# Eight stages of a graph and expert network on one core: beginnings of the stages rearranged

## The reference

```
x = x + gnn0(layernorm(x));  x = x + ffn0(layernorm(x))     # graph convolution; 8 experts, top 2, capacity 187
x = x + gnn1(layernorm(x));  x = x + ffn1(layernorm(x))     # graph attention, batch norm; 8 experts, top 1
x = x + gnn2(layernorm(x));  x = x + ffn2(layernorm(x))     # two attention layers; one expert merged from 8
x = x + gnn3(layernorm(x));  x = x + ffn3(layernorm(x))     # mean of neighbours; 32 experts, each takes its 39 best rows
```

## Time and profile before

| | us |
|---|---|
| median of 3 runs (3417.18 to 3420.14) | 3418.47 |
| the profiled execution | 3384.64 |
| its span, first to last instruction | 3382.9 |
| PE busy | 2479.7 (73%) |
| DVE busy | 1791.0 (53%) |
| ACT busy | 774.3 (23%) |
| POOL busy | 615.5 (18%) |

### The profile page before, as it was taken

How to read it: one execution, slowest core, us unless ns; L and a number is a source line. 1 busy time by engine, 2 the same in 40 slices (tenths; PEclk the granted TensorE clock), 3 DMA queues, 4 the chain that set the end, 5 groups by cost and what they waited for, 6 DMA issues and landing times. The chain is left out here.

```text
span 3382.9 us, 30454 instructions
## 1 busy us (share of the span) xinstructions
PE 2479.7 (73%) x10413; PEld 1584.3 (47%) x10413; DVE 1791.0 (53%) x3838; ACT 774.3 (23%) x1704; POOL 615.5 (18%) x565
## 2 busy tenths in 40 slices
PE   4766940699956888874758999999965486267675
PEld 1334430699954777753423554455432232244342
DVE  9999339322313888875128996199316415221111
ACT  2000100111101667642112651166120000010010
POOL 0000067253001454520110000000002010012111
PEclk9999955799987788885879999999977798588787
DMA  3000234267643555513443542155140203559996
GB/s 120 1 1 13 111 81 142 80 214 242 224 147 97 153 155 149 151 37 137 121 153 128 178 152 77 55 176 174 46 135 0 103 6 106 189 161 315 302 291 177
DMA packets 198763, 447.98 MB, mean 132 GB/s; under 512 B 26116, under 2 KB 47367, under 8 KB 198131
## 3 DMA queue, kind: packets, MB, share of 16 engines
q1 hardware_dynamic: 154963, 344.57, 30.0%
q0 software_dynamic: 43648, 101.46, 11.9%
HBM read 399.26 MB, written 49.05 MB: 133 GB/s over the span
## 5 line engine op out<-in xcount | busy, mean ns | idle before, releaser
L1917 PE MATMUL psum<-x_res,HH 125*128 125x512 f32 (+1 forms) x960 | 352.3, 526 | 20.1 <-DVE x_res L2107 20.1
L1917 PEld LDWEIGHTS psum<-x_res,HH 125*128 125x128 f32 x960 | 181.6, 193 | 179.9 <-issue 156.5
L165 PE MATMUL psum<-ident,ln_xn 125*128 125x125 f32 x320 | 72.0, 381 | 262.0 <-DVE ln_xn L151 261.4
L905 POOL DMA_INDIRECT recd<-edge_records,edge_slots x160 | 191.8, 1199 | 348.9 <-issue 348.9
L1263 POOL DMA_INDIRECT hg<-HT,srcidx x196 | 193.9, 989 | 273.6 <-PE psum L1383 134.4
L1424 ACT ACTIVATE hg<-hg,ex 128x129 f32<-128x129 f32 x784 | 235.2, 388 | 1.6
L1383 PE MATMUL psum<-hg,Dh 128*125 128x258 f32 x784 | 229.8, 457 | 4.8 <-DVE ACC L1326 1.9
L2611 PE MATMUL psum<-wd,hT 128*40 128x512 f32 (+1 forms) x704 | 181.0, 677 | 66.8 <-DMA bdb<-in_L_ffn_b_down 66.3
L1907 PE MATMUL psum<-W,XO 128*125 128x512 f32 x480 | 207.4, 592 | 0.0
L1383 PEld LDWEIGHTS psum<-hg,Dh 128*125 128x125 f32 x784 | 175.6, 230 | 44.9 <-issue 4.8
L165 PEld LDWEIGHTS psum<-ident,ln_xn 125*128 125x128 f32 x320 | 51.4, 196 | 287.1 <-DVE ln_xn L151 160.2
(11 more groups left out here) (418 smaller groups left out, 4097.0 us busy)
## 6 DMA issues: line engine op xcount, KB each, us to landing
wd<-in_L_ffn_W_down SPq DMA_DIRECT2D x32, 2560.0 KB
w<-in_L_ffn_w SPq DMA_DIRECT2D x64, 1024.0 KB, 15.1
MK<-CT SPq DMA_DIRECT2D x80, 625.0 KB
wu<-in_L_ffn_W_up SPq DMA_DIRECT2D x8, 2730.0 KB, 18.8
rows<-ROWS POOLq DMA_DIRECT2D x24, 625.0 KB, 7.3
w<-in_L_ffn_W SPq DMA_DIRECT2D x18, 512.0 KB
t<-in_L_ffn_tv_W SPq DMA_DIRECT2D x16, 512.0 KB
MK<-MASK SPq DMA_DIRECT2D x2, 3125.0 KB, 10.8
```

The costliest lines, as they stand in the source:

```text
L165: ins = pe.transpose(g.PS[:, u, c * 128:c * 128 + TP], self.xn[u][:, c * 128:(c + 1) * 128], g.ident[0:TP, 0:TP])
L905: pool.indirect_dma_start(out=g.recd, out_offset=bass.IndirectOffsetOnAxis(ap=g.posi[:, c:c + 1], axis=0), in_=g.E8[:, c, :], in_offset=No ...
L1917: return pe.matmul(flat[:, at:at + x1 - x0], HH[:, k, h * DH + c * 128:h * DH + c * 128 + 128], z[n % 4][:, x0:x1], start=(k == 0 and i < ...
```

## The change

The statistics of a tile are taken by tile_statistics where the tile of x is made, at the ends of prepare, ffn1, gnn2 and gnn3, and the next stage's dve_statistics takes only those that are not known. In the loops of Norm.dve_program and of gnn3, load k+2 stands before take k. With XN, DVE normalizes straight into XN. dve_logits waits for the router's loads after the statistics; in ffn0 the router's loads are issued before b1 and b2; in gnn3 loads 0 and 1 stand before the wait for the vectors. The clearing of Y is issued by POOL at the beginning of gnn3, and the copy of x to out in three parts in gnn3, each when its group of tiles is finished.

```diff
+def tile_statistics(g, t):
+    g.known.add(t)
+    g.nc.vector.bn_stats(g.ln_st[:, t, :], g.X[:, t, :]).then_inc(*g.sigs["ln_dve_steps"].up())
 ...
+    def rows(self, k):
+        return self.XN[0:TP, k, :] if self.XN is not None else self.xn[k % 2][:]
 ...
         for t in range(NT):
-            dve.bn_stats(self.st[:, t, :], g.X[:, t, :]).then_inc(*v.up())
+            if t not in g.known:
+                tile_statistics(g, t)
+        g.known.clear()
 ...
     def dve_load(self, k):
-        if k >= 2:
+        if k >= 2 and self.XN is None:
             dve.wait_ge(*self.turned.at(k - 1))
             if self.dram is not None:
                 dve.wait_ge(*self.stored[u].at(16 * (k // 2)))
-            if self.XN is not None:
-                dve.wait_ge(*self.copied.at(k - 1))
-        dve.tensor_scalar(self.xn[u][:], ...
+        dve.tensor_scalar(self.rows(k), ...
 ...
-        ins = act.activation(self.tile(k), pt, ACT.Copy)
-        if self.XN is not None:
-            act.wait_ge(*self.normed.at(k + 1))
-            ins = act.activation(self.XN[:, k, :], self.xn[u][:], ACT.Copy)
-        ins.then_inc(*self.copied.up())
+        act.activation(self.tile(k), pt, ACT.Copy).then_inc(*self.copied.up())
 ...
     def dve_program(self, take):
         self.dve_load(0)
+        self.dve_load(1)
         for k in range(NT):
-            if k + 1 < NT:
-                self.dve_load(k + 1)
+            if k + 2 < NT:
+                self.dve_load(k + 2)
             take(k, k % 2)
 ...   prepare, ffn1, gnn2: at the end of the loop over the last tiles
-            dve.wait_ge(*fc_in.at(NT))
+                dve.wait_ge(*fc_in.at(t + 1))
+                tile_statistics(g, t)
 ...   Router.dve_logits
+        self.norm.dve_statistics()
         dve.wait_ge(*self.loaded.at(32))
-        self.norm.dve_statistics()
 ...   ffn0, sp_program
+            rt.sp_program()
             sp.dma_start(b1r[:], ...
             sp.dma_start(b2b[:], ...
-            rt.sp_program()
 ...   gnn3, pool_program
+            pool.memset(none[:], 0.0).then_inc(*cleared.up())
+            pool.wait_ge(*cleared.at(1))
+            pool.dma_start(g.Y..., none[:, None, :].to_broadcast([TP, NT, D])).then_inc(*zeroed.up(16))
             pool.wait_ge(*vectors.at(48))
             pool.wait_ge(*norm.normed.at(NT))
             pool.tensor_tensor(g.X[:], g.X[:], cst[:, 2:3, :].to_broadcast(full), ALU.add).then_inc(*beta_in.up())
+            for i, (t0, t1) in enumerate(ag.GROUPS):
+                pool.wait_ge(*done.at(i + 1))
+                pool.dma_start(rows[:, t0:t1, :], g.X[:, t0:t1, :]).then_inc(*kept.up(16))
+            pool.wait_ge(*zeroed.at(16))
 ...   gnn3, end of dve_group
+            dve.nop().then_inc(*done.up())
+            for t in range(t0, t1):
+                tile_statistics(g, t)
 ...   gnn3, dve_program
             norm.dve_statistics()
+            norm.dve_load(0)
+            norm.dve_load(1)
             dve.wait_ge(*vectors.at(48))
-            norm.dve_program(dve_take)
+            for k in range(NT):
+                if k + 2 < NT:
+                    norm.dve_load(k + 2)
+                dve_take(k, k % 2)
 ...   ffn3, pool_program
-            pool.memset(none[:], 0.0).then_inc(*cleared.up())
-            pool.wait_ge(*cleared.at(1))
-            pool.dma_start(g.Y..., none[...]).then_inc(*zeroed.up(16))
-            pool.dma_start(out..., g.X[:]).then_inc(*kept.up(16))
             rt.norm.store(pool)
 ...
-            pool.wait_ge(*kept.at(16))
-            pool.wait_ge(*zeroed.at(16))
+            pool.wait_ge(*kept.now())
```

More of the change, by code:

```diff
@@ L111, in __init__ @@
         self.g, self.XT, self.XN, self.dram = g, XT, XN, dram
-        self.st, self.mv = s.sb("ln_st", [TP, NT, 6]), s.sb("ln_mv", [TP, NT, 2])
+        self.mv = s.sb("ln_mv", [TP, NT, 2])
         self.rs = s.sb("ln_rs", [TP, NT])
-        self.xn = [s.sb(f"ln_xn{u}", [TP, D]) for u in range(2)]
+        self.xn = None if XN is not None else [s.sb(f"ln_xn{u}", [TP, D]) for u in range(2)]
         self.xT = None if XT is not None else [s.sb(f"ln_xT{u}", [128, KC, TP]) for u in range(2)]
@@ L164, in pe_turn @@
         for c in range(KC):
-            ins = pe.transpose(g.PS[:, u, c * 128:c * 128 + TP], self.xn[u][:, c * 128:(c + 1) * 128],
+            ins = pe.transpose(g.PS[:, u, c * 128:c * 128 + TP], self.rows(k)[:, c * 128:(c + 1) * 128],
                                g.ident[0:TP, 0:TP])
@@ L559, in dve_program @@
             dve.wait_ge(*made.at(3))
-            first = v.count - v.base
             for t in range(NT):
@@ L570, in dve_program @@
                                          ALU.add).then_inc(*v.up())
-            dve.wait_ge(*v.now())
+                dve.wait_ge(*v.now())
+                tile_statistics(g, t)
         def act_take(k):
@@ L2371, in ffn2, with gnn3 @@
         pool_program()
-def gnn3(g, Ws, Wn, bias, gamma, beta):
+def gnn3(g, out, Ws, Wn, bias, gamma, beta):
     nc = g.nc
@@ L2385, in gnn3 @@
         beta_in, var, root = s.sig("beta_added"), s.sig("radicand"), s.sig("root")
+        none, cleared = s.sb("none", [TP, D]), s.sig("cleared")
+        done, zeroed, kept = s.sig("tiles_done"), s.sig("zeros_stored"), s.sig("x_to_out")
         norm, ag = Norm(g, s), Aggregate(g, s, H)
@@ L2416, in pool_program @@
         def pool_program():
+            pool.memset(none[:], 0.0).then_inc(*cleared.up())
+            pool.wait_ge(*cleared.at(1))
+            pool.dma_start(g.Y.rearrange("(t p) d -> p t d", p=TP),
+                           none[:, None, :].to_broadcast([TP, NT, D])).then_inc(*zeroed.up(16))
             pool.wait_ge(*vectors.at(48))
@@ L2419, in pool_program @@
             pool.tensor_tensor(g.X[:], g.X[:], cst[:, 2:3, :].to_broadcast(full), ALU.add).then_inc(*beta_in.up())
+            rows = out.rearrange("(t p) d -> p t d", p=TP)
+            for i, (t0, t1) in enumerate(ag.GROUPS):
+                pool.wait_ge(*done.at(i + 1))
+                pool.dma_start(rows[:, t0:t1, :], g.X[:, t0:t1, :]).then_inc(*kept.up(16))
+            pool.wait_ge(*zeroed.at(16))
         def dve_take(k, u):
@@ L2493, in ffn3 @@
         hT, wo = s.sb("hT", [128, FM, SG]), g.X[0:SL, 0:2 * GS, :]
-        none = s.sb("none", [TP, D])
-        kept, listed, gathered = s.sig("x_to_out"), s.sig("slots_listed"), s.sig("gathered0")
+        kept, listed, gathered = g.sigs["x_to_out"], s.sig("slots_listed"), s.sig("gathered0")
         lu = [s.sig(f"w1_loaded{u}") for u in range(2)]
@@ L2545, in pool_program @@
         def pool_program():
-            pool.memset(none[:], 0.0).then_inc(*cleared.up())
-            pool.wait_ge(*cleared.at(1))
-            pool.dma_start(g.Y.rearrange(x_rows, p=TP), none[:, None, :].to_broadcast([TP, NT, D])).then_inc(*zeroed.up(16))
-            pool.dma_start(out.rearrange(x_rows, p=TP), g.X[:]).then_inc(*kept.up(16))
             rt.norm.store(pool)
@@ L2648, in dve_program @@
             dve.nop().then_inc(*listed.up())
-            dve.wait_ge(*kept.at(16))
+            dve.wait_ge(*kept.now())
             for i in range(NG):
@@ L2715, in program @@
                                              "ln_b", "tv_W1", "tv_b1", "tv_W2", "tv_b2", "tv_ln_g", "tv_ln_b")])
-        gnn3(g, *[A["L3_gnn_" + n] for n in ("W_self", "W_neigh", "bias", "gamma", "beta")])
+        gnn3(g, out, *[A["L3_gnn_" + n] for n in ("W_self", "W_neigh", "bias", "gamma", "beta")])
         ffn3(g, out, *[A["L3_ffn_" + n] for n in ("W_router", "b_router", "W_up", "b_up", "W_down", "b_down")])
```

14 lines of the change are left out of this document (7 added, 7 removed).

## The result

The changed kernel takes 3341.9 us (median of 4 runs, 3340.4 to 3342.3), the kernel before 3419.1 beside it (3417.2 to 3420.1): a ratio of 0.977, with a 95% interval of 0.976 to 0.979, or 77 us less. Forecast were 3313.5 and 105 less. The time lies inside the range of 3301 to 3345, near its slow end, but 28 us of the gain are missing, and it lies outside the 3302 to 3325 that the forecast itself claimed with 0.60: it fell where rivals 1 and 3 had it.

What follows compares the result with a forecast made beforehand. The prediction took barrier-parted stages as the bound, the largest piece ffn3's 50.5 us stall behind POOL's clearing and copy; -57 (ffn3) -15.8 (ffn0) -16.5 (ffn1) +1.4 -17.0 (gnn3) = -105, so 3418.5 becomes 3313.5, range 3301 to 3345.

Steps and rivals of the forecast that it cites:

- Rival 1: ffn3: with weights in full flow a round of stores takes 15 us or more; gain 31, not 57; 3340; chance 0.12.
- rival 3: Gain given back: ffn3's prefetch ends too late, or gnn3's clearing delays its loads, losing 17; 3330 to 3345; chance 0.08.
- ffn3, -57: Beginning of ffn3: stores no longer behind clearing and copy; last router products at T+39 against T+95.7; gain 57 us.
- Rivals 1, 4 and 5: ffn3: 1 slow stores (3340, 0.12); 4 weight stream makes the stall (3495, 0.03); 5 stores still blocked (3355, 0.03).
- gnn3, -17.0: gnn3: earlier PE start 5.1, eight holes gone 14.7, less 2.8 at its end; gain 17.0 us, bounds 8 and 19.
- the 5.1 and 14.7: gnn3: 5.1 us from loads not waiting for the vectors, 14.7 from eight holes of 1.84 us before transposes.
- My bound of 8: gnn3: lower bound of the gain, 8 us, if the clearing slows W and the vectors by 9 us.
- ffn1, -16.5: ffn1's router loop: wait 4.74, eight holes of 0.73 (5.8) and a rising clock (6, bounds 0 and 8); gain 16.5 us.
- rival 2: ffn1: the clock stays down; 3319.5 us; chance 0.13.
- ffn0, -17.2: ffn0's router loop: third tile at 448.6 instead of 459.5, then 2.62 us a tile, ending 470.8 against 487.95; gain 17.2.
- the forecast of nothing at gnn2 and ffn2: Early statistics save nothing there: the next step waits for a DMA anyway; the two boundaries together +1.4 us.
- The offset of 33.8 us: Median of timed runs (3418.5) above the profiled execution (3384.6); the gain worked out in profiled time was taken off the median.

Runs made afterwards that it cites:

- copy_back: Changed kernel with the clearing of Y and the copy of x to out back at the head of ffn3's POOL program; ratio to the kernel before 0.9863.
- both: Changed kernel with gnn3's clearing put behind the vectors and its copy of x to out issued by SP; ratio to the kernel before 0.9701.
- clear_late: Changed kernel with POOL clearing Y in gnn3 only once bias, gamma and beta have landed; ratio to the kernel before 0.9726.
- copy_by_sp: Changed kernel with the three parts of gnn3's copy of x to out issued by SP, not POOL; ratio to the kernel before 0.9745.
- loop_back: Changed kernel with load k+1, not k+2, ahead of take k in the routers' loops and gnn3; ratio to the kernel before 0.9854.
- turns_first: Changed kernel with the ten transposes of ffn1 and ffn2 in a row, router products behind them; ratio to the kernel before 0.9756.
- four_buffers: Changed kernel with four buffers instead of two for the normalized rows in ffn0 and ffn3; ratio to the kernel before 0.9709.
- stats_back: Changed kernel with all statistics taken at the beginnings of the stages again; ratio to the kernel before 0.9756.
- before_again: The kernel before, unchanged, profiled a second time; 3411.4 us.
- order_back: Changed kernel with b1 and b2 of ffn0 loaded ahead of the router again; ratio to the kernel before 0.9759.

## Why the prediction was right, and where it was not

The time came out inside the range, but not by the sum. The largest term was right, and most of the mechanisms behind the others; but one term (gnn3) failed almost whole, another (ffn1) lost what it had taken for the clock, and the range held the result only because it had been drawn wide enough for rivals 1 and 3 too. That part is luck. Rival 1's 3340 is near the result, but its mechanism did not occur; rival 3, with its 0.08, gives 3330 to 3345 for the loss that did occur in gnn3.

*ffn3, -57: right.* Measured are -56.1 to the first up product and -62.0 for the stage. The third tile was to come before T+13 (T+10.7), the first up product near T+81 (T+81.3). The sum that gave T+39 for the last router products has two misses that cancel. A round takes 6.7 to 7.4 us, not 8.5, so the four take 28.6 instead of 34; but 7.3 us follow the load that ends the last round (2899.3 to 2906.6: another tile still waits for its store, and the products of three tiles remain), where the sum had 2. That POOL's queue made the stall is shown by copy_back. Rivals 1, 4 and 5 fall with a first round of 7.4 us. The prefetch gave nothing back (rival 3's first half): the body's wait for the down products fell from 66.3 to 56.4, and the body is 6 us shorter, which the forecast did not have and no run explains.

*gnn3, -17.0: the step that failed.* The mechanism behind the 5.1 and 14.7 is right (PE starts 4.7 us earlier; each of the eight holes was worth 2.06 and not 1.84), and copy_back and both show a gnn3 of 183.5 and 182.0, a gain of 19.6 and 21.1. Two costs of the clearing and the copy were mis-sized or missed. The vectors "may land up to 6 us later": they landed 13.9 later, worth 12.3 (clear_late). The 2500 KB of the clearing came on top of 2798 KB of loads, and it was the vectors, issued last, that waited for them. And I looked at the copy's last part only as something ahead of the stores in POOL's queue, never at what the barrier waits for: 7.2 us (copy_by_sp). My bound of 8 for a clearing that delays the loads held the first cost alone (copy_by_sp, which has only that one, gains 9.0); with both the gain was 1.8. This is the second half of rival 3, and it came true beside the forecast.

*ffn1, -16.5, with 6 for the clock: the clock stayed down,* as rival 2 had it. The wait and the holes came as worked out, the holes a little larger: the last logits come 11.7 us earlier, 7.0 of them by the order of the loads (loop_back), where the forecast without the clock had 10.5 and 5.8. I took gnn1's transposes as the model of this loop and left the router products between them out. In turns_first the clock rises to 2.4 GHz in a row of transposes (0.50 until 1588, 1.00 in 1594 to 1596) and falls to 0.50 while only router products run (1598 to 1600). The Trainium skill (TensorE: Matmul & The Clock Gate, Part 4: PE-mode transpose) has transposes as not counting for the clock; the trace of turns_first disagrees, at least for these float32 ones. So the rule gave the right time for this loop by the wrong reason.

*ffn0, -17.2: a size.* Measured is -12.5. POOL was not late, as forecast, and the third tile came at T+13.0 against T+12.0 in the sum (12.5 in what was to be seen), 1.0 late. The pace was 2.96 us a tile (from 450.87 to 471.57, seven tiles), not 2.62: I had taken 4.7 us from a tile's load to its buffer's release from one store of the kernel before, and here it was 4.2 to 6.3. That is 2.4 us; four_buffers shows that it was the stores. The last 1.4 are the end: behind the last load stand its transposes and the products of two tiles, 5.2 us (471.57 to 476.78), for which the sum had one tile, half a microsecond and the 0.7 by which it starts at 449.3 and not at 448.6: 3.8.

*Statistics:* the forecast of nothing at gnn2 and ffn2 is right, for the reason given (waits of 8.11 and 30.48 where 1.60 and 17.95 stood). In ffn0 and ffn3 I had counted them as gains without asking what else covered them; stats_back shows nothing in ffn0, and 2.5 to 4 us up to ffn3's first up product. They were no term of their own, so the sum didn't suffer.

*The offset of 33.8 us:* taking the difference off the median was right, though the prediction gave no reason for it; by the groups of runs it was gnn1.

In all: of 105 forecast, 77 came; gnn3 lacks 15.2, ffn1 6.1, ffn0 4.7, gnn2 and ffn2 3.9, and ffn3 brought 5.0 more. That makes 24.9, against 105 - 80.3 = 24.7 in the profiles. The 3.9 lie within what the stages wander by: before_again, unchanged, has 729.4 for gnn2, 0.7 less than the changed kernel. In gnn2 the products behind the wait for the bias row ran at a lower clock (0.50 and 0.81 in the first two windows of 4 us, 1.00 before) and took 10.9 us in place of 8.6. The longer wait alone does not explain it: in stats_back the wait is 2.15 us, and the clock was 0.63 behind it as well, the products taking 10.3.

## What to carry to other kernels

Moving a transfer a stage ahead is free only if nothing in that stage's first microseconds waits for loads that it delays, and if its landing isn't the last thing that the closing barrier waits for. Here it helped to put it behind the stage's own loads (12.3 us), and to issue it from the queue that the barrier did not wait for (7.2 us, some 2 to 3 of them given back in the next stage). Where a small loop stores each tile from one of two buffers, ask first what a store takes to land; here two more buffers were worth 21 us, and all edits to the order of the routers' loops and loads some 14 (7.0 in ffn1, 1.6 in ffn0 and 0.5 in ffn3 by loop_back, 4.8 in ffn0 by order_back). Work taken off a stage's beginning is worth what the next DMA of that stage leaves of it, and that wait can be read in the timeline before anything is built.

## What the runs showed of the hardware that was not expected

- A barrier waited for the DMA that POOL had under way (7.29 us, until 0.4 us after its landing; 7.28 in clear_late and in four_buffers), and not for the one that SP had issued about 1.5 us earlier (0.32 us).
- TensorE without a hole is not TensorE at full clock: 20 us of transposes and router products in turn at 0.50 (ffn1, and ffn3 in four_buffers), and a fall from 1.00 to 0.50 within router products alone, while transposes alone had raised it (turns_first).
- One stage, gnn1, took 536 to 575 us in the same code, alike within a group of runs on one chip, while gnn2 (726.7 to 732.4) and ffn2 (181.9 to 184.2) did not move with it. Whether it is the chip or something else about the group, the runs do not tell apart.
